# First attention of an eight-stage kernel: output weights loaded, rounded and turned sooner, and the first steps of GpSimd, ScalarE and TensorE in another order

## Chip, cores and metric

One core of one Trainium2 chip. The metric is device time of one execution in microseconds (us), the median of several runs. Times of single instructions are from one profiled execution.

## What is computed

Eight residual stages on x of 1024 tokens by 256 numbers (16 sequences of 64), all in float32: cross attention and feed-forward in turn, four times. Only the first is touched by the change:

```python
def _qdq(x):
    s = jnp.maximum(jnp.max(jnp.abs(x), axis=-1, keepdims=True) / 127.0, 1e-08)
    return jnp.clip(jnp.round(x / s), -127.0, 127.0) * s
q = _qdq(x) @ _qdq(wq).T + bq            # x: the layer-normed input
kv = cond @ wkv.T + bkv                  # cond: the context
k, v = jnp.split(kv, 2, axis=-1)         # then 16 heads of 16
attn = jax.nn.softmax(jnp.einsum('bnhd,bmhd->bhnm', q, k) * scale, axis=-1)
o = jnp.einsum('bhnm,bmhd->bnhd', attn, v).reshape(B, N, C)
out = _qdq(o) @ _qdq(wp).T + bp          # wp: the output weights; x = x + out
```

## The kernel before

All stages are one program. Each engine has its own list of instructions, written out by hand, and the lists are tied together by semaphores; nothing reorders them. The first attention is `attention_qdq` (L364). It works on 8 tiles of 128 tokens, that is two sequences each, and every tile passes through all five compute steps below. The names of the steps are those of the small functions inside, and the same name on two engines is a step and its follow-up.

For a tile t:
- VectorE takes layer norm statistics (`ln_stats_dve`, L266 to L268). GpSimd raises the variance to -0.5 (`rstd`, L274). Tiles 0 and 1 are normalised by VectorE (L285), tiles 2 to 7 by GpSimd (`centred`, L454). VectorE then rounds the rows to 8 bits in five instructions (`qdq_dve`, L345 to L352: maximum, scale, reciprocal, round, scale back). `bias` on GpSimd (L462) adds the output bias `bp` to x in place, and for tiles from 2 on its semaphore `x_pre` is what VectorE waits for before it rounds.
- TensorE turns the rows (`turn`, L674), ScalarE copies them (`rows`, L338), TensorE makes queries, ScalarE adds their bias (L595). `keys` (TensorE L358 from the context) are spread by ScalarE to block form (L587). `values` are computed by TensorE (L700), copied by ScalarE (L617), and GpSimd adds their bias (`value_bias`, L447).
- `scores` (TensorE L714) fill four banks; VectorE takes row maxima and subtracts them (`maxima`, L501 and L502), ScalarE takes exponentials (`exps`, L602), TensorE turns them (L722), ScalarE copies (L608), TensorE multiplies with the values (`outputs`, L735).
- VectorE divides and rounds the outputs (L508, L509, L345 to L348), TensorE turns them (L743), ScalarE copies (L623), TensorE multiplies with the output weights (`result`), VectorE adds to x (L516).

The lists run skewed: a trip i of the loop holds the exponentials of tile i, scores and values of tile i+1, keys and turned rows of tile i+2. Only the start of the stage, ahead of the loop and in its trips 0 and 1, is special: the query weights and the output weights are rounded there too (`query_weights`, `out_weights` on VectorE), turned on TensorE (`weights(w, b)`, L663, in bank `O`) and copied by ScalarE (L572 for query weights, L574 for output weights). TensorE uses bank `O` for the outputs too, so it waits for that copy (`w_sb`) before `outputs`.

Loads go through SP's queue in the order written (`sp`); the output weights, the value bias and the output bias share the semaphore `wp_ld`, at the end of that order. Expert weights of the next stage follow at once behind them.

## Time and profile before

| | |
|---|---|
| time, median of 3 runs | 1075.37 us (1074.51, 1075.37, 1078.58) |
| the profiled execution | 1073.97 us, span 1072.2 us |
| TensorE busy | 982.0 us, 92% of the span |
| VectorE, ScalarE, GpSimd busy | 49%, 30%, 22% |
| mean granted TensorE clock | 0.951 of full speed |
| first attention | from the start to about 90 us |
| TensorE busy in us 0 to 20, 20 to 40, 40 to 60 | 9.64, 13.89, 19.40 us |

The times of runs and the span are of the whole program. In the lists of the trace a time is in us from the start of the span; a row stands for one instruction or several alike in sequence (xN), with its start, the time that it took, engine, source line, operation and, in brackets, how long the engine was idle before it and what ended that wait. PE is TensorE, DVE VectorE, ACT ScalarE, POOL GpSimd. `big` is one large buffer that holds most tiles of the stage, `bank` the PSUM, `xs` and `xT` normalised and turned rows.

### The profile page before, as it was taken

The numbers are of one execution on the slowest core, as the hardware profiler recorded it, in microseconds if no ns is written. First come the engines' busy times: TensorE is split into PE (matmuls) and PEld (weight loads), VectorE is DVE, ScalarE is ACT, GpSimd is POOL, SyncE is SP. The second block draws the span as 40 slices with busy tenths as digits, with TensorE's granted clock in tenths as the row PEclk, the third lists the DMA queues.
The fourth block names the chain that finished last, engine by engine and source line by source line (L and its number), as shares of the span: only waits on it lengthen the run. The fifth ranks groups of instructions, "written<-read, shape, count | busy, mean of one in ns | idle before, by whom it ended". The sixth has DMA issues, their size and how long they took to land.

```text
span 1072.2 us, 18452 instructions
## 1 busy us (share of the span) xinstructions
PE 982.0 (92%) x7228; PEld 694.7 (65%) x7228; DVE 525.7 (49%) x1264; ACT 321.7 (30%) x620; POOL 233.5 (22%) x322
## 2 busy tenths in 40 slices
PE   5888999989999999969765899999959999999999
PEld 4776599546667666658644799999823434354477
DVE  5786523445344353455376121212158787748541
ACT  4672133242121221214310211112114566743100
POOL 5431442420000000003520222222152443400000
PEclk9996999999999999999995899999967999999999
DMA  9103033221011010026002766666320300020000
GB/s 286 46 2 109 11 98 95 83 61 31 15 40 40 26 41 6 12 88 216 1 24 78 287 235 213 222 225 221 133 65 27 158 2 1 1 79 0 1 15 25
DMA packets 39996, 88.95 MB, mean 83 GB/s; under 512 B 4712, under 2 KB 27592, under 8 KB 36584
## 3 DMA queue, kind: packets, MB, share of 16 engines
q1 hardware_dynamic: 32520, 73.60, 20.0%
q0 software_dynamic: 4080, 11.15, 3.7%
q10 hardware_dynamic: 3312, 3.02, 0.8%
q8 instruction: 60, 0.98, 0.4%
q14 instruction: 24, 0.20, 0.1%
HBM read 76.35 MB, written 11.40 MB: 82 GB/s over the span
## 4 chain that ended last, share of the span: by engine, by line
PE 79%; DVE 11%; DMA 3%; issue 2%; ACT 2%; POOL 2%; SPq 1%; DVEq 0%; ACTq 0%; POOLq 0%
PE bank L358 25%; PE bank L1323 10%; PE bank L1342 7%; PE bank L1667 6%; PE bank L2389 5%; PE bank L2435 3%; PE bank L2414 3%; PE bank L2859 3%; PE bank L1313 3%; PE bank L1678 2%; PE bank L1643 2%; PE bank L2453 1%; PE bank L2865 1%; DVE big L2244 1%; DMA big<-yg,big 1%
## 5 line engine op out<-in xcount | busy, mean ns | idle before, releaser
L358 PE MATMUL bank<-XNT,big 128*128 128x512 f32 x296 | 135.0, 606 | 1.5 <-ACT XNT L1481 0.8
L1323 PE MATMUL bank<-big 128*128 128x128 f32 x1012 | 118.5, 277 | 0.1
L1323 PEld LDWEIGHTS bank<-big 128*128 128x128 f32 x1012 | 116.5, 194 | 0.6 <-issue 0.5
L2389 PE MATMUL bank<-big,xs 32*128 32x512 f32 x256 | 88.6, 733 | 12.6 <-DVE xs L285 10.6
L358 PEld LDWEIGHTS bank<-XNT,big 128*128 128x128 f32 x296 | 54.8, 192 | 63.2 <-issue 59.6
L274 POOL TENSOR_TENSOR rstd<-ve,half 128x1 f32<-128x1 f32 x48 | 27.8, 582 | 299.4 <-DVE ve L268 299.2
L2244 DVE TENSOR_REDUCE big<-bank 128x2 f32<-128x512 f32 x128 | 82.0, 685 | 20.7 <-PE bank L2389 20.1
L1342 PE MATMUL bank<-big 128*128 (+1 forms) x368 | 87.3, 380 | 1.1 <-DVE big L1108 0.7
L1101 DVE TENSOR_TENSOR big<-big,bank 128x640 f32<-128x640 f32 x23 | 18.9, 822 | 136.7 <-ACT big L1211 136.7
L2335 ACT ACTIVATE big<-bank 128x1024 f32<-128x1024 f32 x64 | 64.9, 1024 | 39.9 <-PE bank L2414 39.6
L1342 PEld LDWEIGHTS bank<-big 128*128 128x128 f32 (+1 forms) x368 | 66.4, 191 | 8.9 <-issue 1.9
L2414 PE MATMUL bank<-big 32*128 32x512 f32 x256 | 69.9, 672 | 1.6 <-POOL big L2189 1.4
L358 PE MATMUL bank<-CTXT,big 128*128 128x512 f32 (+1 forms) x192 | 68.0, 501 | 0.0
L1667 PE MATMUL bank<-big 128*128 128x256 f32 x256 | 63.1, 392 | 1.5 <-issue 1.2
L358 PE MATMUL bank<-big,CTXT 128*128 128x256 f32 (+1 forms) x224 | 57.9, 410 | 0.0
L1667 PEld LDWEIGHTS bank<-big 128*128 128x128 f32 x256 | 46.7, 193 | 13.4 <-DVE X L1520 5.9
L1526 DVE COPY big<-bank 128x512 f32<-128x512 f32 x16 | 11.1, 691 | 89.2 <-PE bank L1652 89.2
L2389 PEld LDWEIGHTS bank<-big,xs 32*128 32x128 f32 x256 | 31.5, 209 | 34.9 <-issue 19.7
L358 PEld LDWEIGHTS bank<-CTXT,big 128*128 128x128 f32 x192 | 34.2, 205 | 30.1 <-issue 30.1
L358 PEld LDWEIGHTS bank<-big,CTXT 128*128 128x128 f32 x224 | 42.6, 190 | 17.2 <-issue 12.9
L983 POOL DMA_INDIRECT yg<-big x23 | 22.7, 986 | 135.4 <-DVE big L1108 135.4
L1574 ACT COPY big<-bank 128x1024 f32<-128x1024 f32 x16 | 16.2, 1012 | 118.9 <-PE bank L1678 118.9
(358 smaller groups left out, 1638.9 us busy)
## 6 DMA issues: line engine op xcount, KB each, us to landing
big<-m_gu SPq DMA_DIRECT2D x23, 1408.0 KB, 6.0
big<-m_d SPq DMA_DIRECT2D x8, 768.0 KB
big<-a_qk SPq DMA_DIRECT2D x16, 256.0 KB, 3.0
yg<-big ACTq DMA_DIRECT2D x23, 128.0 KB, 2.0
big<-m_gu SPq DMA_DIRECT2D x8, 352.0 KB
big<-a_o SPq DMA_DIRECT2D x16, 128.0 KB, 2.1
xn<-XNT SPq DMA_DIRECT2D x8, 256.0 KB, 2.1
big<-f_keys SPq DMA_DIRECT2D x1, 2048.0 KB, 10.8
```

What stands on the lines that cost most here:

```text
L274: e.tensor_tensor(k.rstd[at % NT][:, :], k.ve[at % NT][:, :], k.half[:, 0:1], ALU.pow).then_inc(k.ln_rstd, 1)
L358: ins = e.matmul(out, a, b, start=start and n == 0, stop=stop and n == len(pairs) - 1)
L1313: ins = e.matmul(bank[:, GU[s % 2], c * F:(c + 1) * F], xgT[s % 2][:, kb, :], WB[:, bass.ds(at[s] + (kb * 2 * F + c * F), F)], start=kb == ...
L1323: ins = e.matmul(gu[:, n if n <= WHOLE else n + 1], gu_slot[s % SLOTS][:, c:c + P], xgT[s % 2][:, kb, :], start=kb == 0, stop=kb == KB - 1)
L1342: ins = e.matmul(bank[:, Y[s % 2], 0:D], hT[s % 2][0:row, b, :], WB[0:row, bass.ds(at[s] + (WGU + b * D), D) if LAG else bass.ds(at[s] * S ...
L1667: ins = e.matmul(bank[:, QK0 + j % 2, q * D:(q + 1) * D], cT[:, t * P:(t + 1) * P], wo[h % 2], start=True, stop=True)
L2244: e.tensor_reduce(nm[t % 2][:, b, c:c + 2 * G:G], k.bank[:, step_bank(step), :].rearrange("p (j n) -> p j n", j=2), AX.X, ALU.max, negate= ...
L2335: e.activation(pt[u % 2][:, r].rearrange("p r j n -> p r (j n)"), k.bank[:, b:b + 2, :], ACT.Exp, scale=float(G) ** -0.5).then_inc(S["ex"], 1)
L2389: e.matmul(bank[:, step_bank(step), :], k.xs[t % 2][q, b * P:(b + 1) * P], cm[t % 2][q, 2 * jp:2 * jp + 2].rearrange("p j n -> p (j n)"), ...
L2414: ins = e.matmul(bank[:, pair_banks(u, pair) + r % 2, :], cr[q, t, jp, nb * P:(nb + 1) * P], xm[t % 2][q, 2 * jp:2 * jp + 2].rearrange("p ...
L2435: ins = e.matmul(bank[r * R:(r + 1) * R, VB, jp * D:(jp + 1) * D], cv[t % 2][:, nb, r * J + 2 * jp + j], pt[u % 2][:, r, j], start=nb == 0 ...
L2859: e.matmul(bank[:, OUT + u % 2, 0:D], hT[:, u // UB, b, c], dn[:, b], start=b == 0, stop=False)
```

## The change

- SP: the load of the output weights `wp` goes ahead of the loads of tiles 2 to 7 of x and of the rest of the context, and has a semaphore of its own, `wo_ld`. `wp_ld` then counts two loads, 32.
- GpSimd: ahead of the loop, `rstd`, centring and then the biases of tiles 0, 1, 2, and then the value bias of tile 0. Before: biases of tiles 0 and 1, value bias of tile 0, `rstd`, centring and bias of tile 2.
- VectorE: `out_weights` takes the half. Half 0 is rounded ahead of the loop, half 1 in trip 0 where both stood.
- ScalarE: the copy of tile 0's values goes from ahead of the loop into trip 0, behind the turned exponentials. The copy of the turned output weights goes from trip 1 to trip 0.
- TensorE: values of tile 0 go behind the turn and the keys of tile 1; the turn of the output weights goes from trip 1 to trip 0, and no longer waits for `o_sb`.

```diff
--- before.py
+++ after.py
@@ -388,7 +388,7 @@
     sw, unround = [A.take(3) for _ in range(KB)], A.take(1)
     per_tile = ("k_ps", "q_ps", "k_sb", "q_sb", "v_ps", "v_cp", "v_sb", "s_ps", "d_sb", "o_ps", "o_sb", "ot_ps",
                 "ot_sb", "y_ps", "x_pre")
-    S = {n: k.sem("a0_" + n) for n in per_tile + ("wq_ld", "wk_ld", "wp_ld", "w_dq", "w_ps", "w_sb", "hd", "p_sb",
+    S = {n: k.sem("a0_" + n) for n in per_tile + ("wq_ld", "wk_ld", "wo_ld", "wp_ld", "w_dq", "w_ps", "w_sb", "hd", "p_sb",
                                                  "pt_ps", "pt_sb")}
     k.give_back([S[n] for n in per_tile], NT)
     k.give_back([S[n] for n in ("p_sb", "pt_ps", "pt_sb")], 2 * NT)
@@ -405,11 +405,11 @@
         e.dma_start(k.CTXT[:, :, 0:2 * P], g["ctxT"][:, :, 0:2 * P]).then_inc(S["wk_ld"], 16)
         e.dma_start(bqk, g["bqk"]).then_inc(S["wk_ld"], 16)
         e.dma_start(wv, g["wvT"]).then_inc(S["wk_ld"], 16)
+        e.dma_start(wn[1], g["wp"]).then_inc(S["wo_ld"], 16)
         xr = g["x"].rearrange("(t p) d -> p t d", p=P)
         e.dma_start(k.X[:, 2:NT, :], xr[:, 2:NT]).then_inc(k.x_tile, 16)
         e.dma_start(k.CTXT[:, :, 2 * P:T], g["ctxT"][:, :, 2 * P:T]).then_inc(k.ctx_ld, 16)
-        for dst, src in ((wn[1], g["wp"]), (bv, g["bv"]),
-                         (bp, g["bp"].partition_broadcast(P))):
+        for dst, src in ((bv, g["bv"]), (bp, g["bp"].partition_broadcast(P))):
             e.dma_start(dst, src).then_inc(S["wp_ld"], 16)
 
     def pool(e):
@@ -441,7 +441,7 @@
 
         def value_bias(t):
             e.wait_ge(S["v_cp"], t + 1)
-            e.wait_ge(S["wp_ld"], 48)
+            e.wait_ge(S["wp_ld"], 32)
             for b in (0, 1):
                 v = vbd[t % 2][:, b, :, :, 0:HD]
                 ins = e.tensor_tensor(v, v, bv, ALU.add)
@@ -458,15 +458,14 @@
 
             if t < 2:
                 e.wait_ge(k.ln_out, at0 + t + 1)
-                e.wait_ge(S["wp_ld"], 48)
+                e.wait_ge(S["wp_ld"], 32)
             e.tensor_tensor(k.X[:, t, :], k.X[:, t, :], bp, ALU.add).then_inc(S["x_pre"], 1)
 
-        bias(0)
-        bias(1)
-        value_bias(0)
         ln_rstd_pool(e, k, at0 + 2, 0)
         centred(2)
-        bias(2)
+        for t in range(3):
+            bias(t)
+        value_bias(0)
         for i in range(NT):
             if i + 1 < NT:
                 value_bias(i + 1)
@@ -489,9 +488,10 @@
         def query_weights(ob):
             qdq_dve(e, ch, wn[0][:, ob], wn[0][:, ob], sw[ob], scaled=False).then_inc(S["w_dq"], 1)
 
-        def out_weights():
-            for ob in range(KB):
-                qdq_dve(e, ch, wn[1][:, ob], wn[1][:, ob], s3[2 + ob]).then_inc(S["w_dq"], 1)
+        def out_weights(ob):
+            if ob == 0:
+                e.wait_ge(S["wo_ld"], 16)
+            qdq_dve(e, ch, wn[1][:, ob], wn[1][:, ob], s3[2 + ob]).then_inc(S["w_dq"], 1)
 
         def maxima(t):
             p = t % 2
@@ -532,6 +532,7 @@
         e.wait_ge(k.x_tile, done0)
         ln_stats_dve(e, k, ch, 2, 0)
         k.dve_strips(e)
+        out_weights(0)
         for i in range(NT):
             maxima(i)
             if i > 1:
@@ -541,8 +542,7 @@
             if i + 2 < NT:
                 normalise(i + 2)
             if i == 0:
-                e.wait_ge(S["wp_ld"], 48)
-                out_weights()
+                out_weights(1)
             if front and i == NT - 1:
                 for t in range(4):
                     front["stats"](e, t)
@@ -627,7 +627,6 @@
         weights(0, O)
         keys(0)
         queries(0)
-        values(0)
         rows(1)
         keys(1)
         for i in range(NT):
@@ -635,13 +634,15 @@
             if i + 1 < NT:
                 queries(i + 1)
             turned(i)
+            if i == 0:
+                values(0)
             if i + 2 < NT:
                 keys(i + 2)
             if i + 1 < NT:
                 values(i + 1)
             if i > 0:
                 out_rows(i - 1)
-            if i == 1:
+            if i == 0:
                 weights(1, O)
             if i + 2 < NT:
                 rows(i + 2)
@@ -757,9 +758,9 @@
         e.wait_ge(S["w_sb"], 1)
         queries(0)
         scores(0)
-        values(0)
         turn(1)
         keys(1)
+        values(0)
         queries(1)
         e.wait_ge(k.ctx_ld, 16)
         for i in range(NT):
@@ -771,8 +772,7 @@
                 values(i + 1)
             if i > 0:
                 out_rows(i - 1)
-            if i == 1:
-                e.wait_ge(S["o_sb"], 1)
+            if i == 0:
                 weights(1, O)
                 e.wait_ge(S["w_sb"], 2)
             outputs(i)
```

VectorE, end of the part ahead of the loop and start of trip 0 (L255 and L256 make strip masks for later stages, L345 to L352 are the rounding, L501 and L502 are maxima and difference of tile 0); one piece of the difference:

```order
 L255 TENSOR_REDUCE strip<-strips 128x4
 L256 TENSOR_REDUCE strip<-strips 128x4
+L345 TENSOR_REDUCE big<-big 128x1
+L346 TENSOR_SCALAR big<-big 128x1
+L347 RECIPROCAL big<-big 128x1
+L348 TENSOR_SCALAR big<-big 128x256
+L352 TENSOR_SCALAR big<-big 128x256
 L501 TENSOR_REDUCE big<-bank 128x16
 L502 TENSOR_TENSOR big<-bank,big 128x1024
```

The five instructions of one half of the output weights stand ahead of the maxima of tile 0; the same five have gone from behind the rounding of tile 2.

ScalarE, from the query biases of tile 0 (L595) to the exponentials of tile 1, before and then after:

```order
L595 ACTIVATE big<-bank,bias,big 128x128 x2
L617 COPY big<-bank 64x16x16 x2
L338 COPY xT<-bank 128x256
L587 ACTIVATE big<-bank,big 128x2x64 x4
L602 ACTIVATE big<-big 128x512 x2
L595 ACTIVATE big<-bank,bias,big 128x128 x2
L608 COPY big<-bank 128x512 x2
L587 ACTIVATE big<-bank,big 128x2x64 x4
L617 COPY big<-bank 64x16x16 x2
L338 COPY xT<-bank 128x256
L602 ACTIVATE big<-big 128x512 x2
```

```order
L595 ACTIVATE big<-bank,bias,big 128x128 x2
L338 COPY xT<-bank 128x256
L587 ACTIVATE big<-bank,big 128x2x64 x4
L602 ACTIVATE big<-big 128x512 x2
L595 ACTIVATE big<-bank,bias,big 128x128 x2
L608 COPY big<-bank 128x512 x2
L617 COPY big<-bank 64x16x16 x2
L587 ACTIVATE big<-bank,big 128x2x64 x4
L617 COPY big<-bank 64x16x16 x2
L574 COPY big<-bank 128x512
L338 COPY xT<-bank 128x256
L602 ACTIVATE big<-big 128x512 x2
```

The value copy of tile 0 (first L617) stands behind the exponentials of tile 0, and the copy of the output weights (L574) ahead of the row copy of tile 2 and the exponentials of tile 1 (last L338 and L602).

TensorE, from the scores of tile 1 on, before and then after (the lines of this function are one higher after the change):

```order
L714 MATMUL bank<-big 64x128 x16
L700 MATMUL bank<-big,CTXT 64x128 x8
L735 MATMUL bank<-big 64x34 x16
L674 MATMUL bank<-ident,xs 128x128 x2
L358 MATMUL bank<-xT,big 128x128 x4
```

```order
L715 MATMUL bank<-big 64x128 x16
L701 MATMUL bank<-big,CTXT 64x128 x8
L664 MATMUL bank<-ident,big 128x128 x4
L736 MATMUL bank<-big 64x34 x16
L675 MATMUL bank<-ident,xs 128x128 x2
L358 MATMUL bank<-xT,big 128x128 x4
```

The four turns of the output weights stand between the values of tile 1 and the outputs of tile 0, ahead of the turn of tile 2.

## Rows read from the trace of the kernel before

**Rows 1.** Timeline of ScalarE: start, us, engine, line, operation, idle before.

```profile
17.59 0.76 ACT L617 COPY big<-bank 64x256 f32<-64x256 f32 x2 [3.00 <-PE bank L700]
...
19.32 1.50 ACT L587 ACTIVATE big<-bank,big 128x128 f32<-128x128 f32 x4 [0.57 <-PE bank L358]
20.70 1.16 ACT L602 ACTIVATE big<-big 128x512 f32<-128x512 f32 x2
...
30.70 1.15 ACT L602 ACTIVATE big<-big 128x512 f32<-128x512 f32 x2 [3.63 <-DVE big L502]
...
37.84 0.58 ACT L574 COPY big<-bank 128x512 f32<-128x512 f32 x1
...
40.27 1.15 ACT L602 ACTIVATE big<-big 128x512 f32<-128x512 f32 x2
```

**Rows 2.** Timeline of VectorE, same columns.

```profile
14.62 0.17 DVE L256 TENSOR_REDUCE strip<-strips 128x4 f32<-128x16 f32 x1
15.76 1.22 DVE L501 TENSOR_REDUCE big<-bank 128x16 f32<-128x1024 f32 x1 [0.97 <-PE bank L714]
...
22.34 0.42 DVE L345 TENSOR_REDUCE big<-xs 128x1 f32<-128x256 f32 x1 [4.10 <-POOL X L462]
...
23.84 0.41 DVE L345 TENSOR_REDUCE big<-big 128x1 f32<-128x256 f32 x1
...
26.55 0.65 DVE L352 TENSOR_SCALAR big<-big 128x256 f32<-128x256 f32 x1
...
28.19 1.22 DVE L501 TENSOR_REDUCE big<-bank 128x16 f32<-128x1024 f32 x1
```

**Rows 3.** Timeline of TensorE, same columns.

```profile
15.57 1.98 PE L700 MATMUL bank<-big,CTXT 128*64 128x128 f32 x16
17.47 0.69 PE L674 MATMUL bank<-ident,xs 128*128 128x128 f32 x2
...
23.66 0.70 PE L714 MATMUL bank<-big 32*64 32x128 f32 x32 [0.20 <-ACT big L608]
...
25.21 1.08 PE L735 MATMUL bank<-big 128*64 128x34 f32 x32
...
31.38 1.44 PE L722 MATMUL bank<-ident,big 128*128 128x128 f32 x8 [3.11 <-ACT big L602]
...
34.46 1.16 PE L714 MATMUL bank<-big 32*64 32x128 f32 x32
...
38.47 1.13 PE L735 MATMUL bank<-big 128*64 128x34 f32 x32 [1.03 <-ACT big L574]
```

**Rows 4.** Chain that ended last: start, us, what.

```profile
6.71 9.00 DMA bias<-bp
...
23.57 0.35 DVE xs L352
```

**Rows 5.** Timeline of GpSimd, same columns.

```profile
15.86 1.41 POOL L462 TENSOR_TENSOR X<-X,bias 128x256 f32<-128x256 f32 x2 [1.37 <-DMA bias<-bp]
...
19.70 0.56 POOL L274 TENSOR_TENSOR rstd<-ve,half 128x1 f32<-128x1 f32 x1
20.36 1.23 POOL L454 TENSOR_SCALAR xs<-X,mv,rstd 128x256 f32<-128x256 f32 x1
...
26.27 1.47 POOL L447 TENSOR_TENSOR big<-big 128x256 f32<-128x256 f32 x2 [3.96 <-ACT big L617]
```

**Rows 6.** Windows: length; busy us by engine, TensorE first; granted clock; DMA share; GB/s.

```profile
16.00:17.00 1.00, 1.00 (x14) 1.00 (x12) 0.98 (x1) 0.00 (x0) 1.00 (x2) 0.50 1.12 350
...
33.00:34.00 1.00, 1.00 (x7) 1.00 (x6) 0.90 (x5) 0.51 (x2) 0.00 (x0) 0.50 0.08 27
```

**Rows 7.** DMA issues of the first 20 us: KB each, us to landing.

```profile
X<-x SPq DMA_DIRECT2D x1, 768.0 KB, 7.6
...
big<-wp SPq DMA_DIRECT2D x1, 256.0 KB, 7.2
```

**Rows 8.** The page: granted TensorE clock in 40 slices, in tenths.

```profile
PEclk9996999999999999999995899999967999999999
```

## The prediction

> **What bounds the kernel now.** I read the stage windows first, then the chain of waits, then the timelines of the four engines over the first 41 us. TensorE is busy for 92% of the span, so in most of the kernel only TensorE work counts; the change moves none of that. It touches the first attention alone, up to its third tile, and there the engines wait for each other. So the question is how much earlier the steady rhythm of that stage begins.
>
> The marks I use are the starts of ScalarE's exponentials (L602) of tiles 0, 1 and 2: **E0 = 20.70, E1 = 30.70, E2 = 40.27** [rows 1]. E0 to E1 takes 10.0 us and E1 to E2 9.57. From E2 on the instruction lists of before and after are the same, so what E2 gains the stage keeps, and with it every later stage, unless something is tied to a fixed moment.
>
> What holds each mark now:
> - E0 is held by ScalarE's own list. VectorE's difference for tile 0 is begun at 15.76 [rows 2] and would allow E0 at about 18.3, but TensorE computes the values of tile 0 (1.98 us) before it turns tile 1 at 17.47 [rows 3], and ScalarE copies values at 17.59 and key blocks at 19.32 [rows 1] first.
> - E1 is held by a long detour. The chain goes from the landing of the output bias (issued at 6.71, 9.00 us under way) [rows 4] over GpSimd: biases at 15.86, then values, `rstd` at 19.70, centring of tile 2 at 20.36 [rows 5]. VectorE stands idle 4.10 us for it until 22.34 [rows 2], then rounds tile 2 and both halves of the output weights before the maxima of tile 1 at 28.19, and E1 follows 2.51 later. TensorE idles 3.11 us behind that [rows 3].
> - E2 is held by TensorE at half clock (granted 0.50, so 1.2 GHz, in the 34th us) [rows 6]: scores of tile 2 take 1.16 against 0.70 for tile 1 [rows 3]. Behind it ScalarE copies the turned output weights at 37.84, and TensorE's outputs of tile 1 wait 1.03 us for that copy, at 38.47 [rows 1, 3]. E2 comes 1.80 after the start of those outputs.
>
> **The change, part by part.**
>
> 1. *SP's queue.* The output weights are issued ahead of two 768 KB transfers, some 1.1 us sooner. Before they took 7.2 us to land, from an issue near 5.2, so about 12.4 [rows 7]; ahead of those two they can only land sooner, and they are wanted at 14.8. The last six tiles of x and the rest of the context come behind 256 KB more: at 350 GB/s [rows 6] that is 0.75 us. x would land near 12.5 instead of 11.7 (7.6 us after an issue at 4.1) [rows 7], and it is read at about 13.5, for the statistics ahead of the strip masks at 14.62 [rows 2]. Cost nothing; the cover is about 1 us, and beyond it each us of lateness is one us on VectorE. Output bias and value bias have the same bytes ahead as before: no change.
>
> 2. *GpSimd.* After the strip masks (read by VectorE at 14.62, [rows 2]) it now does `rstd` and centring of tile 2 at once: `rstd` to centring takes 0.66, centring 1.23 [rows 5], so 14.5 to 16.4. The output bias has landed at 15.7 by then. Three bias additions of 0.7 end at 18.5; tile 2 is ready 3.8 us sooner. The values' bias of tile 0 comes behind, and its data comes only at 23.6 (below): nothing waits.
>
> 3. *VectorE.* Half the output weights now stand ahead of the maxima of tile 0. Five such instructions take 1.50 us (22.34 to 23.84) [rows 2]; from 14.83 they end at 16.33 instead of the 15.76 at which the maxima start now. But GpSimd is centring just then. A 256-wide scale of this sort took 0.65 where it met a GpSimd addition (at 26.55, GpSimd from 26.27), against 0.35 alone [rows 2, 4, 5]. If a scale must let the running GpSimd instruction end, the first (due 15.67) runs at about 16.3 to 16.65, the second waits for a bias addition to 17.3, and the maxima start at 17.55. The bounds are 16.33 and 17.55; I take 17.55, since in the row at 26.55 the wait is just what was left of the addition. The Trainium skill, "SBUF — State Buffer", part "SBUF: two separate sides", says that a VectorE instruction in a two-port mode and a GpSimd instruction take one pair of ports in turn, each for its whole length. That speaks against putting these scales beside the centring, and the row at 26.55 agrees; by it the maxima start at 17.55, without it at 16.33.
>
> 4. *E0.* With the maxima at 17.55 and 2.51 behind them: 20.06. ScalarE's side: TensorE turns tile 1 at 15.57 instead of 17.47 (the values now go behind). From the turn to ScalarE's key blocks it is 1.85 us now (17.47 to 19.32), up to 0.6 more since all of it falls into the stretch at half clock [rows 3, 6]; they take 1.38, so ScalarE is free between 18.8 and 19.4. VectorE is later, so **E0 = 20.06, gain 0.64**; without the collision 19.4, gain 1.3.
>
> 5. *E0 to E1.* Scores of tile 1 follow E0 by 2.96 (20.70 to 23.66, [rows 1, 3]), ScalarE's turned copies end some 0.15 before: 22.86. Its list is then values of tile 0 (0.76), key blocks (1.38 to the next start), values of tile 1 (0.76), output weights (0.58) [rows 1]: 26.34. TensorE's values of tile 1 and the four turns of the weights (rounded by 22.9 on VectorE) are done by 25.4, under it. Now TensorE's outputs of tile 0 wait for that copy, as those of tile 1 do today: start 26.4, and E1 = 26.4 + 1.80 = **28.2**. VectorE would allow sooner: tile 2 rounded from 20.0, weights' second half, statistics, maxima of tile 1 at 23.8, difference done at 26.3. So the new holder of E1 is the row copy of tile 2 on ScalarE, which stands ahead of the exponentials, behind TensorE's outputs. Interval 8.1 for 10.0: gain 1.9.
>
> 6. *E1 to E2.* Scores of tile 2 at E1 + 2.96 + 0.2 (queries of tile 2 are only just begun at E1): 31.4. Then values and two turns to the outputs of tile 1: 1.55 as from 23.66 to 25.21 [rows 3], plus 0.4 for the turns: 33.4. No weights in between any more. E2 = 33.4 + 1.80 = **35.2**. VectorE ends the difference of tile 2 near 34.7, GpSimd has tile 3 ready near 29.6: both under it. 7.0 for 9.57: gain 2.6, of which the weights' turn and wait are 1.6 and the half clock and the long idle the rest.
>
> Sum: 0.64 + 1.86 + 2.57 = **5.1 us**. The profiled execution took 1073.97 (span 1072.2) and would take 1068.9. It stands 1.40 below the median of the three runs, 1075.37, so as a median I expect **1070.3**.
>
> **The rivals.** A measurement of this kernel can tell about 0.5%, 5.4 us, from no change.
>
> - *B, half clock again.* TensorE is at half clock in the 17th us, after a sparse start, and in the 34th after its 3.11 us wait [rows 3, 6]. In the new order it waits some 1.0 us for the weights' copy around 25.7 and does little matmul work until 28.5. For a drop: work there is sparse, as ahead of the first such stretch. Against: no wait of over 1.2 us is left. If a half-clock stretch still lies on queries, turns, key blocks and scores of 28 to 32, it costs 0.46 on scores [rows 3] and about as much again on key blocks, 1.3 in all: 3.8 gained, 1071.6. The Trainium skill, "TensorE: Matmul & The Clock Gate", Part 1, says that the gate's window runs free of the kernel's start; by that, one run may fall in this case and the next not, which no row here shows.
> - *C, no collision.* The scales pass GpSimd, or GpSimd is later: E0 at 19.4, 5.8 gained, 1069.6. For it: only one row shows a scale beside a GpSimd addition, none beside a centring. Against: the two stand side by side in the new order whatever the bias does.
> - *D, given back.* The stage ends 5 us sooner, but what follows doesn't move along: the fourth of 40 slices, where the expert stage starts, has a granted clock of 0.6 [rows 8], and if its half-clock stretch doesn't come forward with the work, 3 to 5 of the 5.1 go: 1074.3.
> - *E, the new wait.* VectorE now waits for the output weights ahead of the maxima of tile 0. Its price is one for one from 14.83 on, since maxima, difference, tile 2 and everything behind wait in its queue. It takes landing after 19.9 to lose all the gain, and after 25.3 to lose a further 0.5%. The output bias, last of the stage's own loads, is under way for 9.00 us [rows 4], which from the new issue at 4.1 would be 13.1; so it would need a queue that serves this one last. If it did, at 26: 6 us slower, 1081.
>
> **How the numbers follow.** Forecast (A) 0.43, B 0.25, C 0.20, D 0.07, E 0.05. A lies 0.3 us short of the 0.5% line. The three runs shown spread by 4 us, most of it upward from the middle one, so perhaps four in ten of A, three quarters of C and one in twenty of B come out over the line: 0.17 + 0.15 + 0.01, rounded up to 0.36 since my sums take no credit for smaller waits that vanish. Slower by over 0.5% is E alone: 0.05. The rest, 0.59, is within. The range takes C with an easy run at its low end (1067.3) and B with 2.5 us of disturbance behind it at its high end (1074.1); part of D and all of E lie outside.
>
> **What would show it.** In the new profile: VectorE's first weight scale near 15.7 stretched to about 0.9 us and the second to about 0.9; maxima of tile 0 near 17.5; no idle of VectorE before tile 2's rounding; E0 near 20.1, E1 near 28.2 behind a row copy, TensorE's outputs of tile 0 waiting for the weights' copy; E2 near 35.2; granted clock 1.00 from 19 to 80; then marks that lie 5.1 earlier to the end of the stage. Maxima at 16.3 say C; a granted clock of 0.50 near 30 says B; VectorE waiting for a DMA at 14.8 says E; a gain at E2 that has shrunk by 100 us says D. The forecast is wrong if E1 stays above 29.5 or E2 above 37.

## The result, and the profile after

| | before | after |
|---|---|---|
| median of 6 runs | 1077.58 us (1074.51 to 1080.29) | 1071.04 us (1069.26 to 1073.05) |
| profiled execution, span | 1073.97, 1072.2 | 1070.49, 1068.7 |
| TensorE busy in us 0 to 90 | 66.38 | 69.69 |
| E0, E1, E2, E3 (ScalarE's exponentials of tiles 0 to 3) | 20.70, 30.70, 40.27, 47.98 | 18.88, 26.98, 34.14, 41.84 |

The ratio is 0.9945, with a 95% interval of 0.993 to 0.996: about 5.9 us less, 4.3 to 7.5. It is not the quotient of the two medians, which lie 6.5 us apart. (The kernel before has a higher median here than ahead of the prediction, because three more runs are in it.) A second comparison of the same two kernels gave 0.9954 (0.994 to 0.9967), 5.0 us (3.5 to 6.5). The forecast was a gain of 5.1 and a median of 1070.3.

ScalarE's timeline after the change, same columns as [rows 1]: start, us, engine, line, operation, idle time before.

```profile
15.77 0.37 ACT L338 COPY xT<-bank 128x256 f32<-128x256 f32 x1 [1.25 <-PE bank L675]
16.66 1.51 ACT L587 ACTIVATE big<-bank,big 128x128 f32<-128x128 f32 x4 [0.52 <-PE bank L358]
18.88 1.15 ACT L602 ACTIVATE big<-big 128x512 f32<-128x512 f32 x2 [0.71 <-DVE big L502]
...
24.54 0.59 ACT L574 COPY big<-bank 128x512 f32<-128x512 f32 x1
26.71 0.37 ACT L338 COPY xT<-bank 128x256 f32<-128x256 f32 x1 [1.58 <-PE bank L675]
26.98 1.15 ACT L602 ACTIVATE big<-big 128x512 f32<-128x512 f32 x2
...
34.14 1.15 ACT L602 ACTIVATE big<-big 128x512 f32<-128x512 f32 x2
...
41.84 1.15 ACT L602 ACTIVATE big<-big 128x512 f32<-128x512 f32 x2 [0.30 <-DVE big L502]
```

E0 waits for VectorE's difference (L502) and no longer for ScalarE's own list. E1 comes 0.27 after the start of the row copy of tile 2, which waited 1.58 us for TensorE's turn. From E2 to E3 it is 7.70; before it was 7.71.

VectorE, to be held against [rows 2]:

```profile
14.76 0.42 DVE L345 TENSOR_REDUCE big<-big 128x1 f32<-128x256 f32 x1
...
15.60 0.35 DVE L348 TENSOR_SCALAR big<-big 128x256 f32<-128x256 f32 x1
15.98 0.48 DVE L352 TENSOR_SCALAR big<-big 128x256 f32<-128x256 f32 x1
16.39 1.20 DVE L501 TENSOR_REDUCE big<-bank 128x16 f32<-128x1024 f32 x1
...
18.76 0.41 DVE L345 TENSOR_REDUCE big<-xs 128x1 f32<-128x256 f32 x1
...
22.82 1.22 DVE L501 TENSOR_REDUCE big<-bank 128x16 f32<-128x1024 f32 x1
...
27.94 0.68 DVE L348 TENSOR_SCALAR big<-big 128x256 f32<-128x256 f32 x1
```

The first scale of the weights, at 15.60, takes 0.35, the second 0.48, and the maxima of tile 0 start at 16.39. The idle time of 4.10 us ahead of tile 2's rounding is gone (it begins at 18.76 with no wait), and the maxima of tile 1 start at 22.82 instead of 28.19. GpSimd, to be held against [rows 5]:

```profile
15.09 1.23 POOL L454 TENSOR_SCALAR xs<-X,mv,rstd 128x256 f32<-128x256 f32 x1
16.30 2.12 POOL L462 TENSOR_TENSOR X<-X,bias 128x256 f32<-128x256 f32 x3
...
27.73 0.74 POOL L462 TENSOR_TENSOR X<-X,bias 128x256 f32<-128x256 f32 x1
```

TensorE, to be held against [rows 3]:

```profile
12.47 1.16 PE L358 MATMUL bank<-xT,big 128*128 128x128 f32 x8 [0.78 <-ACT big L572]
...
15.29 0.44 PE L675 MATMUL bank<-ident,xs 128*128 128x128 f32 x2
...
23.49 0.66 PE L664 MATMUL bank<-ident,big 128*128 128x128 f32 x4
25.18 1.13 PE L736 MATMUL bank<-big 128*64 128x34 f32 x32 [1.03 <-ACT big L574]
```

The wait of 3.11 us for the exponentials of tile 1 is gone. The 1.03 us wait for the weights' copy is still there, one tile sooner, at 25.18. No stretch at half clock lies in the first 80 us of this execution.

What the first stage gains, later stages keep only in part in this one profile. The stores of the normalised tiles, at the start of the expert stage, begin 6.1 us sooner (before, then after):

```profile
L939 SPq DMA_DIRECT2D xn<-big x8: 319/432/452, 84.5 to 93.5; - x8
```

```profile
L939 SPq DMA_DIRECT2D xn<-big x8: 320/426/455, 78.4 to 87.4; - x8
```

The fourth of 40 slices shows a granted clock of 0.6 in this profile too, but the half clock moved along with the work: it sets in in the 81st us instead of the 87th, and the marks stay 6.1 apart until about 200 us. Further on the two executions differ by chance. At 220 us the changed one falls to half clock where the one before did not (windows: length, busy us of the five engines with TensorE first, then granted clock, DMA share, GB/s; before, then after):

```profile
220.00:225.00 5.00, 4.49 (x21) 2.36 (x19) 3.64 (x11) 2.46 (x5) 1.57 (x2) 1.00 0.18 36
```

```profile
220.00:225.00 5.00, 4.22 (x7) 1.89 (x7) 0.00 (x0) 1.28 (x3) 0.00 (x0) 0.66 0.07 26
```

The first matmul of the large expert stage (L1323) starts at 593.1 instead of 595.7, so 2.6 of the 6.1 are left there, and the spans differ by 3.5. Profile against profile the change is thus worth 3.5 us and in the runs 5.9 or 5.0; another pair of profiles of the same two kernels (`e0_before_again` and `e4_change_again`, spans 1076.7 and 1069.5) would say 7.2. One pair of executions is not a measurement of 5 us. The marks of the first stage can be compared, if TensorE's speed at the start is the same in both, which only the experiments showed.

### The profile page after: what moved, and what is told of

It reads as the page before. It is cut to its first block, busy times and chain, and to the rows that moved or that the text cites. A ratio compares the mean times of both kernels' runs of the same rounds, so it can differ in the third digit from the quotient of the medians.

```text
span 1068.7 us, 18450 instructions
## 1 busy us (share of the span) xinstructions
PE 980.7 (92%) x7228; PEld 693.9 (65%) x7228; DVE 526.0 (49%) x1264; ACT 322.0 (30%) x620; POOL 233.8 (22%) x322
## 4 chain that ended last, share of the span: by engine, by line
PE 78%; DVE 12%; ACT 3%; issue 2%; DMA 2%; POOL 2%; DVEq 0%; ACTq 0%; POOLq 0%
PE bank L358 23%; PE bank L1323 11%; PE bank L1342 7%; PE bank L1667 6%; PE bank L2389 5%; PE bank L2414 3%; PE bank L2435 3%; PE bank L2859 3%; PE bank L1313 3%; PE bank L1678 2%; PE bank L1643 2%; PE bank L2453 1%; PE bank L2865 1%; DMA big<-yg,big 1%; DVE big L2244 1%
## 5 line engine op out<-in xcount | busy, mean ns | idle before, releaser
L1323 PE MATMUL bank<-big 128*128 128x128 f32 x1012 | 118.5, 277 | 0.1
L1323 PEld LDWEIGHTS bank<-big 128*128 128x128 f32 x1012 | 116.5, 194 | 0.6 <-issue 0.5
L1101 DVE TENSOR_TENSOR big<-big,bank 128x640 f32<-128x640 f32 x23 | 18.9, 822 | 136.6 <-ACT big L1211 136.6
```

What stands on the lines that cost most here:

```text
L1323: ins = e.matmul(gu[:, n if n <= WHOLE else n + 1], gu_slot[s % SLOTS][:, c:c + P], xgT[s % 2][:, kb, :], start=kb == 0, stop=kb == KB - 1)
```

## The experiments

The theory was that of the prediction: each mark is set by what stands ahead of it in one engine's list, so it can be added up from rows. The rival: the gain comes mostly from where the stretches at half clock happen to fall, which the two profiles suggest too, since the one before has two such stretches in the first 40 us and the one after none.

All marks, in us. Q0 is the start of TensorE's queries of tile 0 (eight passes), and "queries" is how long those take. Where they take 1.16 the start is called fast below, where they take 2.08 slow; in the first profile of the kernel before and in `e5_values_undone` they took 1.16, but half clock set in at about 15.5. The ratios of e5 to e8 come from another chip than those of the other experiments, each against runs of the kernel before on the same chip.

| kernel | Q0, queries | E0 - Q0 | E1 - E0 | E2 - E1 | E3 - E2 | E2 - Q0 | ratio (interval) |
|---|---|---|---|---|---|---|---|
| before, first profile | 12.55, 1.16 | 8.15 | 10.00 | 9.57 | 7.71 | 27.72 | |
| e0_before_again | 12.97, 1.16 | 6.60 | 10.60 | 10.71 | 7.70 | 27.91 | 0.9995 (0.9981 to 1.0008) |
| e11_before_third | 13.08, 2.08 | 9.46 | 9.91 | 9.58 | 7.71 | 28.95 | single run |
| the change, first profile | 12.47, 1.16 | 6.41 | 8.10 | 7.16 | 7.70 | 21.67 | 0.9945 (0.993 to 0.996) |
| e4_change_again | 12.51, 2.08 | 7.97 | 8.27 | 7.16 | 7.71 | 23.40 | 0.9954 (0.994 to 0.9967) |
| e1_gpsimd_alone | 12.61, 2.08 | 9.60 | 6.27 | 8.78 | 7.70 | 24.65 | 0.9967 (0.9954 to 0.998) |
| e2_values_alone | 12.62, 1.16 | 5.56 | 15.67 | 10.39 | 7.71 | 31.62 | 1.0051 (1.0032 to 1.0071) |
| e3_weights_alone | 12.55, 1.16 | 6.67 | 8.61 | 6.84 | 7.71 | 22.12 | 0.9972 (0.996 to 0.9984) |
| e5_values_undone | 12.58, 1.16 | 8.16 | 7.96 | 8.46 | 7.71 | 24.58 | 0.9966 (0.995 to 0.9982) |
| e6_both_halves | 12.47, 2.08 | 8.56 | 8.10 | 7.17 | 7.70 | 23.83 | 0.994 (0.9922 to 0.9959) |
| e7_load_undone | 12.44, 2.08 | 7.97 | 8.80 | 7.16 | 7.71 | 23.93 | 0.9927 (0.9907 to 0.9947) |
| e9_centre_twice | 12.63, 2.08 | 8.36 | 8.09 | 7.16 | 7.71 | 23.61 | single run |
| e8_copy_ahead | 12.46, 2.08 | 7.97 | 7.35 | 7.63 | 7.23 | 22.95 | 0.9924 (0.9905 to 0.9943) |
| e10_tile3_ahead | 12.58, 2.08 | 7.97 | 7.32 | 7.16 | 7.70 | 22.45 | 0.9935 (0.9913 to 0.9957) |

### TensorE's speed at the start

The changed kernel, unaltered, once more.

> The changed kernel once more, for its spread. If the marks are set by the lists, E0 18.9, E1 27.0 and E2 34.1 come again within 0.3 us or, if a half-clock stretch falls on the keys of tile 1 (none did in the first profile), E0 later by up to 0.6. By the clock theory E2 differs from the first profile by 1 us or more. Time 5.0 to 6.5 us under before.

E0 came at 20.48 and not at 18.9, E1 at 28.75 and E2 at 35.91, 1.8 us later than in the first profile of the same program. TensorE's rows say why:

```profile
12.51 2.08 PE L358 MATMUL bank<-xT,big 128*128 128x128 f32 x8 [0.78 <-ACT big L572]
15.57 1.16 PE L715 MATMUL bank<-big 32*64 32x128 f32 x32 [0.99 <-ACT big L595]
...
17.14 1.91 PE L358 MATMUL bank<-CTXT,big 128*128 128x128 f32 x8
18.99 1.60 PE L701 MATMUL bank<-big,CTXT 128*64 128x128 f32 x16
```

The same eight passes of tile 0's queries take 2.08 instead of 1.16, scores 1.16 instead of 0.70, keys 1.91 instead of 1.06: about half speed from 12.5 to about 19. The same passes take 2.08 in `e2_values_alone` at 28.58, where the granted clock is 0.50. The windows give a granted clock of 1.00 here all the way from 12 to 20 us, as they do in all eight slow starts, so the column doesn't tell and only the durations do. Taken as it was put ahead of this run, an E2 more than 1 us off was the sign of the rival: the clock does move all marks of one program by 1.8 us. But it does so ahead of E0. Behind E0 the differences come again: 8.27 and 7.16.

So the kernel before was run again too.

> The kernel before once more. The other runs showed that E0 depends on how fast TensorE is between 12.4 and 19: the eight passes of tile 0's queries took 1.16 or 2.08 us. If that is a state of the execution and not of the kernel, this one too lands in one of three places: E0 near 19.2 (fast throughout), near 20.7 (half clock from 15.5) or near 22.2 (slow from 12.4). The lists fix the differences whatever E0 is: E1 - E0 = 10.0, E2 - E1 = 8.8 without a half-clock stretch near 33, 9.6 to 10.1 with one. If the clock made the change's gain, E1 - E0 would come out near 8.

> The kernel before a third time, one look, for a further state of the start: E1 - E0 = 10.0 and E2 - E1 between 8.8 and 10.1 again.

All three places turned up: with TensorE fast throughout (E0 - Q0 6.60), at half clock from 15.5 as in the first profile (8.15), slow from 12.4 on (9.46). E1 - E0 was 10.60, 10.00 and 9.91, never near 8: as the main cause the rival falls. (The 10.60 is not the clock, which reads 1.00 there until 30 us. E1 hangs on the copy of tile 0's values, through GpSimd, and comes 13.1 to 13.2 behind it in all three: 16.93, 17.59 and 19.25.) E2 - E1 was 10.71 in the fast start, with a granted clock of 0.50 from 30 to 37 us (it had been put at up to 10.1), and 9.58 in the slow one. Compared between starts of the same TensorE speed, the change gains at E2 6.2 us (27.91 against 21.67, fast) and 5.6 us (28.95 against 23.40, slow). Q0 itself moves by 0.6 us between executions, which is why the marks are taken from there.

A part of these two gains is the rival's all the same. All three profiles of the kernel before have a half-clock stretch between E1 and E2, beside TensorE's wait of 3.0 to 3.7 us; `e1_gpsimd_alone` below, with the same work between E1 and E2 and no such stretch, takes 8.78. By that, a rough estimate, half clock holds 1.9 of the 6.2 (10.71 - 8.78) and 0.8 of the 5.6 (9.58 - 8.78), and the lists 4.3 and 4.8.

### The three parts one by one

GpSimd's order alone:

```diff
-        bias(0)
-        bias(1)
-        value_bias(0)
         ln_rstd_pool(e, k, at0 + 2, 0)
         centred(2)
-        bias(2)
+        for t in range(3):
+            bias(t)
+        value_bias(0)
```

> Only GpSimd's order is changed: rstd, centring and biases of tile 2 ahead of the value bias of tile 0. By the list theory (each mark is set by what stands ahead in one engine's list) E0 stays at 20.7, since ScalarE still copies the values of tile 0 first; VectorE no longer idles 4.1 us, rounds tile 2 from about 18.4, and E1 falls to about 27.0, now held by the row copy of tile 2 behind TensorE's outputs of tile 0. The output weights still stand in trip 1, so E2 is about 35.8, a gain of 4.5 us. By the clock theory (what moved is mostly where half-clock stretches fall) E1 and E2 follow the granted clock of this run: with a half-clock stretch near 32 E2 comes near 37.1, and E1 would gain under 2 us.

This start was slow, so E0 is 22.21; behind it 6.27 and 8.78 stand where 6.3 and 8.8 had been expected. E2 - E0 is 15.05, even less than the 15.26 of the whole change.

The move of tile 0's values alone (TensorE and ScalarE):

```diff
@@ scalar
         queries(0)
-        values(0)
         rows(1)
...
             turned(i)
+            if i == 0:
+                values(0)
@@ tensor
         scores(0)
-        values(0)
         turn(1)
         keys(1)
+        values(0)
```

> Only the values of tile 0 are moved, on TensorE behind the keys of tile 1 and on ScalarE behind the turned exponentials of tile 0. By the list theory E0 falls by 2.4 us to about 18.3, but GpSimd still has the value bias of tile 0 at the head of its list, whose data now comes at 21.8 instead of 18.4; tile 2 is ready at 25.7 instead of 22.3, E1 comes near 34.1 and E2 near 43.7: slower by 3.4 us than before. By the rival (an early E0 is kept) E2 falls by 2.4 us to 37.9 and the kernel is faster by 2.

E0 - Q0 falls to 5.56, the smallest of all, and the kernel is slower: 1.0051, 5.5 us (3.4 to 7.6). VectorE's timeline shows the price:

```profile
15.66 1.22 DVE L501 TENSOR_REDUCE big<-bank 128x16 f32<-128x1024 f32 x1 [0.42 <-PE bank L715]
...
25.60 0.42 DVE L345 TENSOR_REDUCE big<-xs 128x1 f32<-128x256 f32 x1 [7.46 <-POOL X L462]
```

The maxima of tile 0 start at 15.66, and then VectorE stands 7.46 us for tile 2, since GpSimd sat in its list at the value bias of tile 0 until 21.70. E2 is 44.24, 4.0 later than before, of which 0.8 is a longer half-clock stretch (E2 - E1 is 10.39 against 9.57; the granted clock is 0.50 from about 26 to 40 us).

The output weights alone (the change, with the values and GpSimd's list put back as before):

```diff
@@ against the change: scalar and tensor as in the kernel before for values(0)
-        ln_rstd_pool(e, k, at0 + 2, 0)
-        centred(2)
-        for t in range(3):
-            bias(t)
+        bias(0)
+        bias(1)
+        value_bias(0)
+        ln_rstd_pool(e, k, at0 + 2, 0)
+        centred(2)
+        bias(2)
```

> Only the output weights are moved: loaded sooner, half rounded ahead of the maxima of tile 0, turned and copied in trip 0. GpSimd's list and the values of tile 0 stand as before. By the list theory E0 stays at 20.7 (the maxima of tile 0 start 0.6 later, under ScalarE's list), tile 2 is still late at 22.3, one rounding of 1.5 us less stands behind it: E1 about 28.9, E2 about 36.1, a gain of 4.2 us. By the rival (the weights were hidden behind the wait for tile 2 and gain nothing) E1 stays near 30.7 and only the 1.6 us of trip 1 are gained.

Start fast, E2 - E0 15.45, expected 15.4. One mark was missed: E0 - Q0 is 6.67 where ScalarE's list was to hold it; in a fast start VectorE holds it with the weights, as in the change, though only by 0.1 us: ScalarE's list would be free at 19.13 and E0 is 19.22.

The change without the move of the values:

```diff
@@ against the change, scalar
         queries(0)
+        values(0)
         rows(1)
...
-            if i == 0:
-                values(0)
@@ tensor
         scores(0)
+        values(0)
         turn(1)
         keys(1)
-        values(0)
```

> The change without its move of tile 0's values: those are computed and copied ahead of the turn of tile 1 as before. By the list theory E0 is back at 20.7, held by ScalarE; E1 about 28.7 (ScalarE's list is 0.76 us shorter behind E0, TensorE's outputs of tile 0 still wait for the weights' copy) and E2 about 35.8: 1.7 us of the change's 6.1 are lost. If instead GpSimd's and the weights' moves carry all of it, E2 stays at 34.1.

E1 - E0 is 7.96 as expected; E2 - E1 is 8.46, not 7.16, because this execution fell to half clock there (windows: length, busy us, granted clock, DMA share, GB/s):

```profile
27.00:30.00 3.00, 2.54 (x39) 2.26 (x40) 1.76 (x6) 1.42 (x3) 2.90 (x4) 0.79 0.75 235
30.00:33.00 3.00, 3.00 (x20) 3.00 (x19) 2.37 (x9) 1.91 (x4) 0.19 (x1) 0.64 0.67 203
```

```profile
28.85 2.07 PE L358 MATMUL bank<-xT,big 128*128 128x128 f32 x8 [0.46 <-ACT xT L338]
30.72 1.74 PE L722 MATMUL bank<-ident,big 128*128 128x128 f32 x8
32.29 1.06 PE L358 MATMUL bank<-CTXT,big 128*128 128x128 f32 x8
```

Without it E2 - E0 would be 15.12. So GpSimd's move and the weights' move are not two gains: alone they give E2 - E0 = 15.05 and 15.45, together 15.12. Both shorten the same stretch, VectorE's work ahead of the maxima of tile 1, and once GpSimd has moved VectorE holds nothing there (it waits for TensorE's scores ahead of those maxima, 0.43 us in e1, 1.47 in e5). What the weights' turn and copy cost then only changes its place: 6.27 + 8.78 with them in trip 1, 7.96 + 7.16 with them in trip 0. The values' move gives 1.5 at E0 in a slow start (9.46 or 9.60 against 7.97) and 0.2 in a fast one, and costs 0.1 to 0.4 behind it (15.26 and 15.43 against 15.05 and 15.12). Alone it costs 4.

The times agree. GpSimd alone, the weights alone and both together lie near one another (0.9967, 0.9972, 0.9966), with intervals that overlap. The order with all three parts is faster than both together: 0.9927 with the load undone (below) against 0.9966, on the same chip, and these intervals don't meet.

### The load

```diff
-        e.dma_start(wn[1], g["wp"]).then_inc(S["wo_ld"], 16)
         xr = g["x"].rearrange("(t p) d -> p t d", p=P)
...
+        e.dma_start(wn[1], g["wp"]).then_inc(S["wo_ld"], 16)
         for dst, src in ((bv, g["bv"]), (bp, g["bp"].partition_broadcast(P))):
```

> The change with the output weights' load back in its old place behind the rest of x and of the context, its own semaphore kept. It landed at 12.4 before and VectorE wants it at 14.8: no mark moves by more than 0.1 us and the time is the change's. If the load's place mattered, VectorE would show a wait for a DMA ahead of the first weight maximum at 14.8, and all marks would be later by it.

VectorE shows no wait for a DMA; E0 - Q0 is 7.97, as in the change after an equally slow start (e4_change_again). The maxima of tile 0 wait 0.35 for TensorE's scores, not for weights. E1 - E0 is 8.80 instead of 8.27, because half speed reached further here, into the queries of tile 1 (from 20.82, over at 22.1). The load's new place does nothing to the marks. The ratio is lower than the change's (0.9927 against 0.9954), on another chip; no mark of this stage explains that.

### Does GpSimd hold up a scale?

```diff
         k.dve_strips(e)
         out_weights(0)
+        out_weights(1)
...
-            if i == 0:
-                out_weights(1)
```

> The change with both halves of the output weights rounded ahead of the maxima of tile 0. The second half's two scales fall at 17.1 and 17.5, beside GpSimd's bias additions (16.3 to 18.4). If a scale waits for a running bias addition, the maxima start at 18.5 to 18.9 and E0 is 21.0 to 21.4; if it doesn't, at 17.9 with E0 20.4. E1 is E0 + 8.1 and E2 is E1 + 7.2 in both. So the kernel is 1.5 (no waiting) to 2.5 us (waiting) slower than the change.

```profile
15.59 0.35 DVE L348 TENSOR_SCALAR big<-big 128x256 f32<-128x256 f32 x1
15.98 0.47 DVE L352 TENSOR_SCALAR big<-big 128x256 f32<-128x256 f32 x1
...
17.19 0.68 DVE L348 TENSOR_SCALAR big<-big 128x256 f32<-128x256 f32 x1
17.90 0.70 DVE L352 TENSOR_SCALAR big<-big 128x256 f32<-128x256 f32 x1
18.53 1.21 DVE L501 TENSOR_REDUCE big<-bank 128x16 f32<-128x1024 f32 x1
```

```profile
15.07 1.23 POOL L454 TENSOR_SCALAR xs<-X,mv,rstd 128x256 f32<-128x256 f32 x1
16.29 2.16 POOL L462 TENSOR_TENSOR X<-X,bias 128x256 f32<-128x256 f32 x3
```

Scales beside the bias additions take 0.68 and 0.70, so the maxima start at 18.53, inside the range for waiting. The one beside the centring takes 0.35. E0 is 21.03, only 0.55 after that of the change with an equally slow start, since there ScalarE's keys held E0 at 20.48; so the kernel is 0.4 us later at E2, not 1.5 to 2.5.

The next kernel has both halves ahead too, and a second centring, into a spare place, where the additions stood (the line that makes the spare place is left out here):

```diff
         centred(2)
+        e.tensor_scalar(spare, k.X[:, 2, :], k.mv[2][:, 0:1], k.rstd[2][:, 0:1], ALU.subtract, ALU.mult)
         for t in range(3):
             bias(t)
```

> Both halves of the output weights ahead of the maxima of tile 0, and GpSimd centres tile 2 a second time into a spare place, so that a centring runs from 15.1 to 17.5 and the bias additions only from there. If a scale is held up only by a two-input addition of GpSimd and not by its centring (one tensor in, one out), the scales at 15.6, 16.0 and 17.1 take 0.35 each and only the last, at 17.5, may take up to 1.0. If any GpSimd instruction holds a scale up, the one at 15.6 takes over 0.9 and the one at 17.1 about 0.7. Nothing else is to be read from its time.

```profile
15.74 0.35 DVE L348 TENSOR_SCALAR big<-big 128x256 f32<-128x256 f32 x1
16.13 0.47 DVE L352 TENSOR_SCALAR big<-big 128x256 f32<-128x256 f32 x1
...
17.34 0.49 DVE L348 TENSOR_SCALAR big<-big 128x256 f32<-128x256 f32 x1
17.87 0.69 DVE L352 TENSOR_SCALAR big<-big 128x256 f32<-128x256 f32 x1
```

```profile
15.23 1.23 POOL L455 TENSOR_SCALAR xs<-X,mv,rstd 128x256 f32<-128x256 f32 x1
16.46 1.23 POOL L467 TENSOR_SCALAR big<-X,mv,rstd 128x256 f32<-128x256 f32 x1
17.66 2.17 POOL L463 TENSOR_TENSOR X<-X,bias 128x256 f32<-128x256 f32 x3
```

The scale at 15.74 lies wholly in a centring and takes 0.35. Those at 16.13 and 17.34 reach across a start of the next GpSimd instruction (16.46, 17.66) and take 0.12 and 0.14 more. The one that begins inside an addition takes twice its time.

That looks as if only the two-input addition held a scale up. But in these two kernels every scale inside an addition begins 0.19 to 0.22 us after its start, and the one inside a centring 0.51 after. Other runs have the missing cases. A scale early in a centring (`e8_copy_ahead` below, then `e1_gpsimd_alone`):

```profile
28.60 1.23 POOL L454 TENSOR_SCALAR xs<-X,mv,rstd 128x256 f32<-128x256 f32 x1
28.75 0.55 DVE L348 TENSOR_SCALAR big<-big 128x256 f32<-128x256 f32 x1
```

```profile
29.73 1.23 POOL L454 TENSOR_SCALAR xs<-X,mv,rstd 128x256 f32<-128x256 f32 x1
29.95 0.48 DVE L348 TENSOR_SCALAR big<-big 128x256 f32<-128x256 f32 x1
```

And one late in an addition (`e5_values_undone`; the second of the two runs from about 19.2 to 19.8):

```profile
18.52 1.32 POOL L447 TENSOR_TENSOR big<-big 128x256 f32<-128x256 f32 x2
19.71 0.35 DVE L348 TENSOR_SCALAR xs<-xs,big 128x256 f32<-128x256 f32 x1
```

So the centring holds a scale up as well, and what counts is how soon behind the start of GpSimd's instruction the scale begins: 0.15 us behind a centring's start it takes 0.55, 0.22 behind 0.48, 0.51 behind 0.35; 0.19 to 0.22 behind an addition's start 0.66 to 0.70, 0.28 behind 0.54 to 0.65, 0.55 behind 0.35. As an estimate from these rows, a scale can't get on for the first 0.35 us of a centring and for about the first 0.5 of an addition (0.15 + 0.55 - 0.35; 0.2 + 0.69 - 0.35), and doesn't wait for the end of either. Why it is so isn't shown, and neither is what the 0.12 to 0.14 are.

### A kernel that beats both in the stage

```diff
@@ tensor
                 scores(i + 1)
+            if i == 0:
+                weights(1, O)
+            if i + 1 < NT:
                 values(i + 1)
...
             if i == 0:
-                weights(1, O)
                 e.wait_ge(S["w_sb"], 2)
@@ scalar
+            if i == 0:
+                weights(1, O)
             if i + 1 < NT:
                 values(i + 1)
             if i > 0:
                 out_rows(i - 1)
-            if i == 0:
-                weights(1, O)
```

> The change, and in trip 0 the turn of the output weights ahead of the values of tile 1 on TensorE, their copy ahead of the copy of those values on ScalarE. TensorE's 1.03 us wait for the copy shrinks to about 0.3: outputs of tile 0 at 24.4 instead of 25.2, E1 26.2 instead of 27.0. By the list theory not all of it arrives at E2: tile 3 comes from GpSimd at 29.0, VectorE's maxima of tile 2 then start at 31.3, so E2 is about 33.9 (0.25 sooner) and E3 about 41.1 (0.7 sooner than 41.84). By the rival that the wait for the copy alone sets the pace, E2 and all later marks are 0.75 sooner; by the one that GpSimd holds everything, E3 is unmoved.

```profile
25.98 1.13 PE L736 MATMUL bank<-big 128*64 128x34 f32 x32 [0.25 <-ACT big L574]
```

The wait for the weights' copy shrinks to 0.25. E1 - E0 is 7.35, E2 - E1 7.63 (expected: 7.3 and 7.7), and E3 - Q0 30.18 against 31.11 in e4_change_again, whose start was as slow: 0.9 us sooner. The time is 0.9924 of before (0.9905 to 0.9943) and was taken on the other chip. Its interval overlaps that of the change (0.994 to 0.9967) and its median is no lower (1071.11 against 1071.05), so the times don't show that it is faster; the marks show it for this stage.

```diff
@@ gpsimd, on top of it
         for i in range(NT):
-            if i + 1 < NT:
+            if 0 < i < NT - 1:
                 value_bias(i + 1)
...
                 bias(i + 3)
+            if i == 0:
+                value_bias(1)
```

> The kernel with the weights' copy ahead, and in trip 0 GpSimd prepares tile 3 (rstd, centring, bias) ahead of the value bias of tile 1. In the run before it VectorE found tile 3 ready only at 30.5, E1 + 2.7, and that held E2 (E2 - E1 = 7.63, against 7.16 in the change). Now tile 3 is ready near E0 + 7.5, so E2 - E1 is 7.16 again, and E3 - E2 7.3 to 7.7. Measured from E0, E3 comes at E0 + 21.8 or so, against E0 + 22.2 with the copy ahead alone and E0 + 23.1 in the change: 1.3 us less in all, which the times cannot resolve with certainty. If GpSimd was not the holder, E2 - E1 stays 7.6.

E2 - E1 is back at 7.16: GpSimd did hold E2. But E3 - E2 is then 7.70 instead of 7.23, and E3 - Q0 is 30.15 against 30.18. I had counted on 0.4 more at E3. The trace shows what holds it (L518 is here VectorE's addition of the result to x):

```profile
35.63 0.48 DVE L518 SCALAR_TENSOR_TENSOR X<-bank,big,X 128x256 f32<-128x256 f32 x1 [1.22 <-PE bank L358]
```

VectorE is early now and waits 1.22 us for TensorE's result of tile 0, which comes 23.05 us behind Q0; in `e8_copy_ahead` that addition starts 23.07 behind Q0, after a wait of 0.15. From it to E3 it is VectorE's own list, 7.10 and 7.11 us. What GpSimd gave at E2 ends in a wait for TensorE.

## Why the prediction held, and where not

- *The end of it* (5.1 us, 1070.3): 5.9 and 5.0 us in two comparisons, 1071.04. In the marks 5.6 (slow start) and 6.2 (fast start) at E2, so 0.5 to 1.1 were missed. Some of the closeness is luck. The forecast of the median started from 1075.37, and over six runs the kernel before stood at 1077.58; and the steps 3 and 4 below were wrong without the sum showing it.
- *Step 1, the load, at nothing*: right, shown by its undoing.
- *Step 2, GpSimd*: centring from 15.1 (forecast 15.2), tile 2 no longer waited for. Right; by the experiments it carries most of the gain behind E0, since this part alone brings E2 - E0 to 15.05, and the 1.6 us that step 6 gave to the weights' turn and wait come back as a cost between E0 and E1 (7.96 against 6.27).
- *Step 3, the collision*: this failed. "I take 17.55" for the maxima of tile 0; measured 16.39 with fast scores, 16.83 behind slow ones. The lower bound of 16.33 was the right one, because the collision cost 0.12 us and not 1.2. The rule was wrong, that a scale lets the running GpSimd instruction end: at 26.55 in the kernel before, from which it was read, about 0.5 of the addition was left (two take 1.47 from 26.27 on, so the first ends near 27.0) and the scale lost 0.30. And the first scale of the change escaped by its place, 0.51 us into the centring; 0.15 into one it takes 0.55. The Trainium skill, "SBUF — State Buffer", "SBUF: two separate sides", lets a VectorE instruction in a two-port mode and a GpSimd instruction share one pair of ports so that whichever starts first holds it for its whole length and the other is blocked. The rows here don't agree with that: a scale with 0.53 us of addition left lost 0.33 (17.19 in `e6_both_halves`), one with 0.72 of centring left lost nothing (15.60 in the change), and the measurement decides. Whether these scales run in a two-port mode no row shows.
- *Step 4, E0*: forecast 20.06, a gain of 0.64. It has no one value. In a fast start the gain is 0.2 (6.60 to 6.41), in a slow one 1.5 (9.46 to 7.97), and 0.64 lies between them by luck. The forecast compared a start with half clock with one that it priced by the same stretch, without asking whether the stretch belongs to the kernel. By the Trainium skill, "TensorE: Matmul & The Clock Gate", Part 1, the gate's window runs free of the kernel's start; the traces fit that, with 1.16 and 2.08 us for the same instructions of the same program, though they don't show the gate itself there (the granted clock reads 1.00).
- *Step 5, E0 to E1*: forecast 8.1, measured 8.10 and 8.27. Holder as named: the row copy of tile 2, behind TensorE's outputs, behind the weights' copy (1.03 us of wait).
- *Step 6, E1 to E2*: forecast 7.0, measured 7.16 in every run of the change without a half-clock stretch.
- *That E2's gain is kept*: E3 - E2 is 7.70 or 7.71 in all of these kernels but one, and the stores of the next stage start 6.1 sooner. Rival D falls for the expert stage. Later on 2.6 us went in one profile by a stretch at 220 us and others. The runs, 5.9 and 5.0 (intervals 4.3 to 7.5 and 3.5 to 6.5), don't show that any of the 5.6 to 6.2 is lost on the average, and can't exclude 1 or 2 us.
- *Rival B, half clock again*: it exists, with the price given: 1.30 (8.46 - 7.16) against 1.3, but it fell on e5_values_undone. The order of the change was profiled three times (twice as it is, once with the load undone), and none of the three had a half-clock stretch between E1 and E2, nor had `e6_both_halves` and `e9_centre_twice`. That the stretch of the kernel before goes away, step 6 had counted, together with the long idle, at the 1.0 which the weights leave of its 2.6; by the estimate above it is 0.8 to 1.9.
- *Rival C, no collision*: true of its price, 5.8 of gain at E2 against 5.6 and 6.2, and nearly of the mechanism: the scales of the change lose 0.12 us. The forecast had given it 0.20; it deserved more than the case with the collision.
- *Rival E, the wait for the weights*: fell; no wait for a DMA stood there even with the load undone. The slower case that does exist was not among the rivals: the values' move without GpSimd's, 4 us.

## What to carry to other kernels

When an engine's list has an item whose data comes late, everything that others need must stand ahead of it; moving the producer later (here tile 0's values) and not the waiting item (GpSimd's value bias) turned 1.0 us of gain at E0 (6.60 to 5.56) into 5.5 us of loss. Parts that shorten the same stretch don't add up: try each alone before crediting it. When two runs seem to separate two kinds of instruction, see whether the instructions also met at different moments. And before a difference of 1 or 2 us between two profiles is explained, look at one and the same program twice, and at how long a fixed group of matmuls takes in each.

## What the runs showed of the hardware

- TensorE's speed in the first 20 us is a matter of the execution: the eight passes of tile 0's queries took 1.16 in six of the 14 profiles of the table and 2.08 in eight, with the same program in both groups (the change, and the kernel before). E0 - Q0 moves with it by 1.6 us in the change (6.41 to 7.97) and by 2.9 in the kernel before (6.60 to 9.46). In the slow starts the granted clock reads 1.00 all the same, up to 20 us, though the passes take as long as at a granted 0.50 (2.08 at 28.58 in `e2_values_alone`).
- A 256-wide scale of VectorE (0.35 us alone) is held up by a GpSimd instruction of 256 columns only in the first part of it. Begun 0.15 and 0.22 us into a centring of 1.23 it takes 0.55 and 0.48, 0.51 into one 0.35. Begun 0.19 to 0.22 into a two-input addition of 0.73 it takes 0.66 to 0.70, 0.28 into one of 0.68 to 0.79 it takes 0.54 to 0.65, 0.55 into one 0.35. In none of these rows did it wait for GpSimd's instruction to end.
- Begun 0.28 to 0.33 ahead of the start of GpSimd's next instruction, with one running before that, it takes 0.47 to 0.49.
